# Reordering every engine's instruction list in a decoder-layer kernel, and splitting the row transfers of the softmax maxima over two queues

## The reference, cut to what matters

```python
x = layernorm(x + attention(x))       # 16 heads of 32, causal softmax, biases, output projection
x = layernorm(x + wkv(x, ctx))        # a recurrence over the tokens, channel by channel
x = layernorm(x + gated_attention(x)) # 16 query heads, one key head and one value head picked per token
```

## Time and profile before

| | us |
|---|---|
| median of 3 runs | 1542.65 (1542.21 to 1544.36) |
| the profiled execution | 1540.05 |
| its span, first to last instruction | 1538.2 |
| PE busy in the span | 1403.6 |
| DVE busy in the span | 1088.6 |
| ACT busy in the span | 647.1 |
| POOL busy in the span | 391.6 |

### The profile page before, as it was taken

How to read it: one execution, slowest core, us unless ns; L and a number is a source line. 1 busy time by engine, 2 the same in 40 slices (tenths; PEclk the granted TensorE clock), 3 DMA queues, 4 the chain that set the end, 5 groups by cost and what they waited for, 6 DMA issues and landing times.

```text
span 1538.2 us, 26567 instructions
## 1 busy us (share of the span) xinstructions
PE 1403.6 (91%) x9858; PEld 1117.2 (73%) x9858; DVE 1088.6 (71%) x2258; ACT 647.1 (42%) x1459; POOL 391.6 (25%) x520
## 2 busy tenths in 40 slices
PE   7877899999999999999999999999999999998686
PEld 6665777877777777778777777777777777775564
DVE  4464777677777767777777777777777777777744
ACT  3442525445352544535353453525345352534122
POOL 1243312222231222213122231313223131312200
PEclk9988999999999999999999999999999999999898
DMA  6431333314133331414233241333324132331110
GB/s 180 151 83 42 90 77 80 94 34 111 45 90 91 80 94 45 112 36 100 78 87 94 54 108 36 90 77 91 90 56 105 39 87 77 91 77 33 32 44 27
DMA packets 63199, 119.50 MB, mean 78 GB/s; under 512 B 14304, under 2 KB 32736, under 8 KB 63072
## 3 DMA queue, kind: packets, MB, share of 16 engines
q1 hardware_dynamic: 60128, 112.03, 29.0%
q10 hardware_dynamic: 2944, 5.77, 1.1%
HBM read 32.81 MB, written 8.39 MB: 27 GB/s over the span
## 4 chain that ended last, share of the span: by engine, by line
PE 62%; DVE 13%; ACT 9%; issue 3%; SPq 2%; DMA 2%; POOL 0%; ACTq 0%; POOLq 0%; DVEq 0%
PE pp L467 7%; PE pp L469 6%; PE pp L468 6%; PE po L572 6%; PE pw L467 4%; PE pw L469 4%; PE pw L468 4%; DVE neg_max L1499 3%; PE po L586 3%; PE po L576 3%; PE sk L545 3%; PE sk L492 3%; ACT prob L1128 3%; PE sq L507 2%; PE sq L492 2%
## 5 line engine op out<-in xcount | busy, mean ns | idle before, releaser
L1128 ACT ACTIVATE prob<-sk 128x512 f32<-128x512 f32 x384 | 215.6, 597 | 274.4 <-PE sk L492 271.5
L1499 DVE TENSOR_REDUCE neg_max<-sq 128x2 f32<-128x512 f32 (+1 forms) x384 | 252.0, 683 | 87.3 <-PE sq L492 83.6
L467 PE MATMUL pp<-xt_hi,w_hi 128*128 128x256 f32 x616 | 190.2, 309 | 12.7 <-DVE w_lo L1486 7.7
L468 PE MATMUL pp<-xt_lo,w_hi 128*128 128x256 f32 x616 | 175.2, 284 | 0.0
L469 PE MATMUL pp<-xt_hi,w_lo 128*128 128x256 f32 x616 | 175.2, 284 | 0.0
L1139 ACT ACTIVATE o_ch<-po 128x512 f32<-128x512 f32 x128 | 76.2, 596 | 162.1 <-PE po L576 160.6
L467 PEld LDWEIGHTS pp<-xt_hi,w_hi 128*128 128x128 f32 x616 | 119.7, 194 | 15.0 <-issue 11.4
L492 PE MATMUL sq<-mask_qk,ident_b 128*128 128x256 bf16 (+1 forms) x384 | 124.7, 325 | 0.0
L492 PE MATMUL sk<-mask_kq,ident_b 128*128 128x256 bf16 (+1 forms) x384 | 124.4, 324 | 0.0
L468 PEld LDWEIGHTS pp<-xt_lo,w_hi 128*128 128x128 f32 x616 | 119.3, 194 | 0.7
L469 PEld LDWEIGHTS pp<-xt_hi,w_lo 128*128 128x128 f32 x616 | 118.7, 193 | 0.0
(11 more groups left out here) (201 smaller groups left out, 3771.7 us busy)
## 6 DMA issues: line engine op xcount, KB each, us to landing
q_stack<-q_hi SPq DMA_DIRECT2D x256, 128.0 KB, 2.4
q_stack<-q_lo SPq DMA_DIRECT2D x128, 128.0 KB, 2.4
k_stack<-k_hi SPq DMA_DIRECT2D x128, 128.0 KB, 2.3
x_raw<-in_xT SPq DMA_DIRECT2D x16, 512.0 KB, 3.8
k_stack<-k_lo SPq DMA_DIRECT2D x64, 128.0 KB, 2.3
x<-in_x SPq DMA_DIRECT2D x16, 512.0 KB, 4.5
w_val<-in_ctxT SPq DMA_DIRECT2D x64, 128.0 KB, 2.2
out_y<-x SPq DMA_DIRECT2D x13, 512.0 KB, 2.8
```

The lines of the kernel that those rows point to most:

```text
L467: T.matmul(out, lh, rh, start=(c == 0), stop=False, skip_group_check=True)
L468: T.matmul(out, lh, rl, start=False, stop=False, skip_group_check=True)
L1128: A.activation(dst, sk[n % 2][:], ACT.Exp, scale=SCALE).then_inc(s_exp, 1)
L1499: V.tensor_reduce(dst, src, AX.X, ALU.max, negate=True).then_inc(s_max, 1)
```

## The change: what it does

It changes these things, and nothing that is computed:

1. **Rows of the maxima.** `row_hi` on ACT, after its copy of the high part, waits for the copy's own completion and issues the DMA of row 96 from ACT's queue. `stack_max` on SP issues row 97 alone.
2. **Passes of the loop.** PA_WO waits for six of the seven jobs, and PA_WO + 1 for the seventh. On PE `max_a(t, 1)` stands behind `sq_a(t, 1, 2)` and `sk_a(t, 0, 2)`, tiles 0 and 1 of `sk_f` ahead of `turn_f(b, 0)`, and `sk_f(b, 0, ...)` is laced in at two places. On DVE `maxima_a(t, 0, 2)` comes ahead of `recurrence_start(r, 2)`, both splits of x2 and the maxima of group 1 change places with their neighbours, and the last residual and the statistics of b - 1 stand behind them. On ACT `carry_exps(r, 2)` comes behind the exponentials of group 0 and the second row, and `exps_f(b, 2, 0, 1)` ahead of `qk_hi`. On SP `max_f(b, 3)` comes ahead of the q stacks of the next batch.
3. **Opening.** Chunks 2 and 3 of the recurrence of batch 0 move into pass 1, as in the other passes. PE issues extra matmuls that nobody reads (`keep`): 20 ahead of the first scores of batch 1, 6 ahead of those of batch 2, and 24 in pass 1. SP stacks k ahead of the context loads.
4. **Ending.** All five lists are written anew: the third sublayer of batch 14 is laced with that of batch 15 from its projections on. `kf_stack` and `logit_t` no longer share memory, the second jobs of batch 15 use `pw` in place of `po`, and the links of batches 14 and 15 have semaphores of their own.

```diff
-            def stack_max(b, g, job, s_mhi, s_free, mrow):
-                wait(sp, s_mhi, NG * b + g + 1)
-                for part in range(2):
-                    if part:
-                        wait(sp, s_free, job + 1)
-                    row = 3 * HD + part
-                    sp.dma_start(q_stack[row:row + 1, ...], max_rows[:, part, :]...).then_inc(mrow[g], 16)
+            def stack_max(b, g, job, s_free, mrow):
+                wait(sp, s_free, job + 1)
+                row = 3 * HD + 1
+                sp.dma_start(q_stack[row:row + 1, ...], max_rows[:, 1, :]...).then_inc(mrow[g], 16)
...
                 A.activation(max_rows[:, 0, :], pt[0:HG * TT, 0:P], ACT.Copy).then_inc(s_mhi, 1)
+                act.wait_ge(s_mhi, done)
+                row = 3 * HD
+                act.dma_start(q_stack[row:row + 1, ...], max_rows[:, 0, :]...).then_inc(mrow[g], 16)
...
                     if job == PA_WO:
+                        wait(pe, pf_free, PF_JOBS * (b - 1) - 1)
+                        pe.wait_ge(a_free, A_JOBS * (b + 1))
+                    if job == PA_WO + 1:
                         wait(pe, pf_free, PF_JOBS * (b - 1))
-                        pe.wait_ge(a_free, A_JOBS * (b + 1))
...
@@ TensorE, iteration
-                sq_a(t, 1, 2)
...
                 sk_a(t, 0, 0, 1)
+                sq_a(t, 1, 2)
+                sk_a(t, 0, 2)
                 max_a(t, 1)
-                sk_a(t, 0, 2)
...
-                    project_a(t, PA_WO + 1, first_scores_f)
+                    project_a(t, PA_WO + 1, {1: first_scores_f, 2: first_scores_f_end})
...
                 def second_scores_f():
                     if f:
+                        sk_f(b, 1, 0, 1)
                         turn_f(b, 0)
                         sq_f(b, 2, 2)
-                        sk_f(b, 1, 0, 1)
                         sk_f(b, 1, 2)
...
@@ ScalarE, iteration
-                if t > 1:
-                    carry_exps(r, 2)
                 value_out(t, 1)
...
                 exps_a(t, 0, 0, 1)
+                exps_a(t, 0, 2)
                 row_hi_a(t, 1)
-                exps_a(t, 0, 2)
-                if t > 1:
-                    now_exps(r, 2)
-                    carry_exps(r, 3)
+                carry_exps(r, 2)
+                now_exps(r, 2)
                 copy_a(t, 0)
-                if t > 1:
-                    now_exps(r, 3)
+                carry_exps(r, 3)
+                now_exps(r, 3)
...
+                if f:
+                    exps_f(b, 2, 0, 1)
                 qk_hi(t + 1, PA_Q + 1)
                 if f:
-                    exps_f(b, 2, 0, 1)
                     exps_f(b, 2, 2)
...
@@ VectorE, iteration
-                if t > 1:
-                    recurrence_start(r, 2)
                 maxima_a(t, 0, 2)
-                if t > 1:
-                    recurrence_start(r, 3)
+                recurrence_start(r, 2)
                 rows_a(t, 0)
-                if b >= 1:
-                    last_third_residual(b - 1, x_of(b - 1))
+                recurrence_start(r, 3)
                 maxima_a(t, 1, 0, 1)
                 if f:
                     x2_split_lo(b, 0)
-                    x2_split_lo(b, 1)
                 maxima_a(t, 1, 2)
+                if f:
+                    x2_split_lo(b, 1)
+                if b >= 1:
+                    last_third_residual(b - 1, x_of(b - 1))
                 if b >= 1:
                     third_stats(b - 1, x_of(b - 1))
                 rows_a(t, 1)
...
@@ SyncE, iteration
                 if b >= 0:
+                    max_f(b, 3)
                     q_stacks(t + 1, PA_JOBS, PA_Q, pa_free, range(NG - 2), f_sk, TILES * b, a_stk)
-                    max_f(b, 3)
...
@@ VectorE, opening
+                qk_lo(1, PA_K)
+                qk_lo(1, PA_K + 1)
                 sums(0, 0)
                 sums(0, 1)
-                recurrence_start(0, 2)
-                qk_lo(1, PA_K)
                 divide(0, 0)
-                qk_lo(1, PA_K + 1)
+                maxima_a(1, 0, 0, 1)
                 divide(0, 1)
-                recurrence_start(0, 3)
-                sums(0, 2)
-                sums(0, 3)
-                divide(0, 2)
-                divide(0, 3)
-                maxima_a(1, 0, 0, 1)
...
@@ TensorE, ending (b is 13, n is 14, then b is 15)
+                project_f(n, PF_Q, lambda: sk_f(b, 2, 0, 1))
...
+                project_f(n, PF_K + 1, lambda: turn_f(b, 3))
+                project_f(n, PF_V)
+                key_transpose(n, f_free, F_JOBS * n)
+                y_transpose(LAST, 1)
...
+                max_f(n, 0)
+                sq_f(n, 1, 0, 1)
+                b = LAST
+                x2_transpose(b)
+                sq_f(n, 1, 2)
...
+                project_f(b, PF_Q, lambda: sk_f(n, 0, 0, 1))
...
+                project_f(b, PF_Q + 1, second_scores)
...
+                project_f(b, PF_K, third_values)
+                turn_f(n, 2)
+                project_f(b, PF_K + 1, lambda: sk_f(n, 3, 0, 1))
+                sk_f(n, 3, 2)
+                project_f(b, PF_V, lambda: values_f(n, 3))
+                turn_f(n, 3)
                 key_transpose(b, f_free, F_JOBS * b)
...
@@ ScalarE, ending, batch 15: new place of the norm and store of batch 14
                 exps_f(b, 1, 2)
                 copy_f(b, 1)
+                third_norm(n, x_of(n))
+                store_whole(n)
                 exps_f(b, 2, 0, 1)
...
@@ VectorE, ending, batch 15
                 rows_f(b, 2)
+                third_stats(n, x_of(n))
                 maxima_f(b, 3)
```

More of the change, by code:

```diff
@@ L221, in build @@
         dve_a, dve_w, dve_f, dve_once = sem("dve_a"), sem("dve_w"), sem("dve_f"), sem("dve_once")
+        dve_f_end = [sem(f"dve_f_end{i}") for i in range(2)]
         pool_w, pool_once, act_once = sem("pool_w"), sem("pool_once"), sem("act_once")
@@ L718, in project_f @@
                 bank = bank_f(b, job)
-                if bank is po and job == PF_Q + 1:
-                    pe.wait_ge(f_norm, NG * b)
                 if bank is pw and job == PF_K + 1:
                     pe.wait_ge(u_free, U_JOBS * (b + 1))
+                    if b == LAST - 1:
+                        pe.wait_ge(w_free, W_JOBS * (b + 1) + W_YJ + 1)
                 else:
-                    if bank is pw and job == PF_V + 1:
+                    if bank is pw and job == PF_V + 1 and not is_last(b):
                         pe.wait_ge(w_free, W_JOBS * (b + 2))
@@ L863, in iteration @@
                 else:
+                    keep(pp, 6)
                     third_values()
+                    keep(pp, 6)
                 turn_a(t, 2)
@@ L953, in iteration @@
                     pe.wait_ge(a_max, TILES * (t + 1))
+                    keep(sq[0], 6)
                 sq_a(t + 1, 0, 0, 1)
@@ L1406, in ending @@
                 row_hi_f(b, 2)
+                carry_exps(LAST, 0)
                 copy_f(b, 1)
-                x2_split_hi(LAST - 1)
-                carry_exps(LAST, 0)
+                x2_split_hi(n)
+                carry_exps(LAST, 1)
                 exps_f(b, 2, 0, 1)
-                carry_exps(LAST, 1)
                 now_exps(LAST, 0)
-                fq_hi(LAST - 1, 0)
+                now_exps(LAST, 1)
+                fq_hi(n, 0)
                 exps_f(b, 2, 2)
-                now_exps(LAST, 1)
+                row_hi_f(b, 3)
                 copy_f(b, 2)
-                row_hi_f(b, 3)
-                fq_hi(LAST - 1, 1)
+                carry_exps(LAST, 2)
+                fq_hi(n, 1)
+                carry_exps(LAST, 3)
                 exps_f(b, 3, 0, 1)
+                now_exps(LAST, 2)
                 exps_f(b, 3, 2)
+                now_exps(LAST, 3)
+                gate_sums(n)
                 copy_f(b, 3)
-                carry_exps(LAST, 2)
-                now_exps(LAST, 2)
-                carry_exps(LAST, 3)
-                now_exps(LAST, 3)
+                row_hi_f(n, 0, f_mrow[NG - 1], 32 * n)
                 third_norm(b, x_of(b))
-                act.wait_ge(x3_ready, b + 1)
-                act.dma_start(out_d[b].rearrange("(c p) d -> p c d", p=P), x_of(b)[:]).then_inc(stored, 16)
-                b = LAST - 1
-                gate_sums(b)
+                store_whole(b)
+                b = LAST
+                x2_split_hi(b)
+                exps_f(n, 0, 0, 1)
+                for stk in f_stk:
+                    act.wait_ge(stk, 48 * b)
+                fq_hi(b, 0)
+                row_hi_f(n, 1)
+                exps_f(n, 0, 2)
+                copy_f(n, 0)
+                exps_f(n, 1, 0, 1)
+                fq_hi(b, 1)
+                exps_f(n, 1, 2)
+                row_hi_f(n, 2)
+                copy_f(n, 1)
+                exps_f(n, 2, 0, 1)
+                exps_f(n, 2, 2)
+                gate_sums(b)
+                row_hi_f(n, 3)
+                copy_f(n, 2)
+                exps_f(n, 3, 0, 1)
+                exps_f(n, 3, 2)
+                copy_f(n, 3)
```

347 lines of the change are left out of this document (157 added, 190 removed).

## The result

The changed kernel takes 1530.33 us (median of 5 runs, 1527.12 to 1533.29) where the one before took 1542.21 beside it (5 runs, 1538.30 to 1544.36): the ratio is 0.9928 [0.9905, 0.9951]. It is faster, by 12 us where I had forecast 47, and the time lies 0.3 us above my range.

What follows compares the result with a forecast made beforehand. PE, busy for 91% of the span, sets the pace, so only its waits can be gained. Loop 28.7, opening 6 and ending 12.5 us take 47.2 off 1540.05; with 2.6 added for the median, 1495.5 us, range 1474 to 1530.

Steps and rivals of the forecast that it cites:

- The loop, forecast 28.7 us: Loop: 2.55 us a pass gained from shorter PE waits, 0.5 charged for ACT, net 2.05 over 14 passes.
- I counted 2.3 of them: Loop waits of PE: 0.5 us a pass off for picked, 1.1 for maxima, 0.7 for exponentials.
- The price of the split: Loop, ACT: issuing high rows there costs 0.5 us a pass on the path, bounds 0 and 5.3.
- The 0.25 us for the rows: Loop: PE's waits for row DMAs shrink by an estimated 0.25 us a pass, the low row starting sooner.
- PA_WO's 0.5 us: Loop: of PA_WO's 1.17 us wait for picked, about 0.5 us a pass is gained; sq limits the rest.
- the waits move, and the loop gains little: Rival, loop: each removed wait shows the next DVE or ACT chain; 7 us instead of 28.7, 1517 us; 17%.
- the signs that I named as wrong: Profile after: sk and po waits for prob above 12 us, new sq waits for maxima, or pass 1 above 47 us.
- the one for ScalarE's issues: Sign in the loop that ACT's issues are on the path: sk and po wait for prob above 12 us.
- The opening, forecast 6: Opening: 7.2 us of waits and 4.3 of clock gained, 4.4 and 1 charged; bounds -2 and 14.
- the 8.7 us of which I took half: Opening: two stretches at 1.2 GHz would save 8.7 us at 2.4; 4.3 counted for keep matmuls and shorter waits.
- The ending and the tail, forecast 14 and -1.5: Ending: 9 us idle time and 5 us clock gained; tail: 1.5 us charged for batch 14's norm, store and statistics.
- The new wait of `pw`: Ending: PF_K + 1 of batch 14 waits 2.7 us for pw, freed after batch 15's second residual; the longest wait.

Runs made afterwards that it cites:

- the split alone: The kernel before the change, with only the high rows issued from ScalarE and SP issuing row 97 alone: 1557.20 us against 1543.50.
- The kernel with the load first: The changed kernel with only load_weight(W_O), the output projection's weights, ahead of the first high row on ScalarE in the opening: 1531.01 us.
- `out_lo` early: The changed kernel with out_lo(t, 0) ahead of divide(r, 2) on DVE: 1508.22 us.
- PA_WO alone: The kernel before the change, with only PA_WO's wait eased to six jobs and the seventh awaited at PA_WO + 1: 1538.92 us against 1543.50.

## Why the prediction was wrong

**The loop, forecast 28.7 us: the term that failed.** Its gains were there. The waits for picked, for exponentials and for the maxima's transposes went, 3.4 us a pass, where I counted 2.3 of them. Three steps in between failed, the first two the largest:

- *An edit that was not costed.* "The change part by part" passes over `sums(r, 2)` and `sums(r, 3)`, each one place back on DVE. I asked of each wait that went whether its own releaser was late, and not what now stood between the last maximum and `k_lo`, which frees the same bank `pt`. Taking `out_lo` out from behind the division, which shortens that chain from 3.96 to 2.31 us, gave back 1.5 us a pass, some 20 us. The scans themselves were not put back, so that their move made the wait is read from the two timelines.
- *The price of the split.* I put 0.5 us a pass on ScalarE's own path, "where `carry_exps` now stand behind the exponentials of group 0". No exponential waits there. It costs 0.68 us a pass net, elsewhere: ScalarE's issue delays `xt_hi`, that POOL's `xt_lo`, that DVE's `v_f`, that the maximum, and that PE. I looked at what PE awaits of ScalarE, not at what POOL awaits. The trace before could have shown it: `v_f` took 0.47 us beside a 0.24 of the same shape. The bounds I gave (0 and 5.3) held it. The 0.25 us for the rows was right, 0.2 measured.
- *PA_WO's 0.5 us.* I had the mechanism, `sq` behind the first maximum. (The 935.05 in that working stands in no row; the maximum's first half ends at 934.97.) Alone it gains 0.34. It counts on a maximum that comes no later, and the split takes that away: with both, `sq` waits 1.7 us.

And one term was missing: the sum has no dips of the clock in the loop. Without the 7.0 us of the three passes that hold one, the loop would have gained a little; with them it lost 3.6.

The rival "the waits move, and the loop gains little" is what came, at a price above its own: it had still left 7 us of gain in the loop. Its reason, DVE without a gap around the picks, was the right row to look at, and 17% was too little for it. Of the signs that I named as wrong, its own came, 22.2 us of new waits of `sq` for a maximum; the one for ScalarE's issues, waits for `prob`, did not.

**The opening, forecast 6, measured 9.4 from the first to the second PA_WO.** The clock (third number from the end in these rows of the two kernels) went from 0.85 to 1.00, so by my working it gave back all the 8.7 us of which I took half (no run shows the clock's part by itself):

```profile
64.50:142.00 77.50, 58.70 (x366) 46.20 (x365) 39.94 (x72) 31.82 (x72) 30.71 (x33) 0.85 0.25 62
```

```profile
69.00:137.00 68.00, 55.54 (x410) 44.91 (x408) 39.45 (x72) 31.77 (x72) 30.18 (x33) 1.00 0.29 71
```

The wait for the first maximum is gone, and that for k is 1.6 us at most (3.2 before). On the other side stand up to 4.4 us before the first PA_WO, which I had at nothing, because the first 65 us have no edit of their own but the split.

**The ending and the tail, forecast 14 and -1.5, measured 17.7 and -8.3.** The sum was 9.4, where I had 12.5. The new wait of `pw` for the second residual of 15 was forecast at 2.7 us and is the longest single one:

```profile
PE pw L483 <- DVE x L1610: 3.5, 1, 3.5
```

In the tail I charged ScalarE's norm and store at 1.5 us. What failed is the size: moving norm and store with the statistics gave 5.3 us, 3.4 by their durations and the rest with a higher clock. The rows on ScalarE, which I had credited there, cost another 1.4 (the means of 48.5 against 47.2 and 48.9 against 47.3). Why they do is not shown: under the old ending the split alone has a tail of 38.7 us, no longer than the 40.2 before. The last 1.6 us stay open.

**The rule I weighed.** The issue on ScalarE takes 0.63 us, within my bounds. The Trainium skill (DMA: Bandwidth & Descriptors, "Issuing engines are not separate DMA queues") says that such a split saves only sequencer time, usually little. The trace agrees on the size: 0.2 us a pass, 2.6 us in 13, where no maximum stands behind it.

## What to carry to other kernels

When a wait is taken out of a full pipeline, list everything else that frees the same bank or feeds the next instruction, on every engine, and ask it of each moved instruction in the diff, the ones that look neutral too. An issue moved to an engine with idle time is not free if something behind it on that engine starts a chain on a third one: follow it until it meets the critical engine again. An instruction that is sometimes longer than the same form elsewhere is a row to explain before it is built upon; and a part that costs, like this split, shows only when the parts are timed alone.

## What the runs showed of the hardware

**A small DVE instruction was held up by a running POOL instruction.** `v_f` (TENSOR_SCALAR, 128x32, fp32) took 0.24 us alone, and 0.47, 1.35 and 1.42 us where it began 1.95, 1.07 and 1.03 us into POOL's `xt_lo` of 2.4 us; in these three it ended 0.04 us after `xt_lo`. In the loop of the changed kernel three more kinds got longer where they began during an instruction of POOL: the TENSOR_TENSOR `k<-k_sel,k` (128x32, 0.19 us alone, 1.17 to 1.28 then), the TENSOR_TENSOR `x<-x,o_tok` (128x256, 0.42 and 0.92) and the scan `w_e<-w_e` (128x256, 0.67 alone, 0.96 to 1.21 then). Two kinds beside `xt_lo` were hardly touched: `picked<-pw`, which reads a bank, took 0.67 us during it and 0.67 to 0.69 elsewhere, and the TENSOR_REDUCE behind it 1.10 us during `xt_lo` and 1.06 outside it (medians of 13 each in the kernel before). The Trainium skill (SBUF — State Buffer, "Who interferes with whom") says that VectorE and GpSimd share one pair of ports, which is held for a whole instruction while the other blocks, and that a tensor_scalar can ask for that pair and a reduction can't. These rows agree. Here a wait on the less busy engine was worth 19 us.

**The clock.** In the loop of the changed kernel the granted clock falls to 1.2 GHz three times (at 487, 846 and 1204 us), and the passes with such a dip are 1.9 to 2.8 us longer than undisturbed ones. The kernel with the load first has three, `out_lo` early one, and in all three kernels `sq` waits 1.7 to 2.0 us in every pass. Each of these seven dips begins 0.2 to 1.7 us after the end of that wait. The wait isn't enough, since 10 of the 13 passes of the changed kernel have it and no dip, and it isn't the only cause: PA_WO alone has one dip, elsewhere in the pass. The kernel before and the other ten runs have none in the loop. The passes without a dip are not all equal either: above the shortest they have 2.1 to 7.8 us in 13 (4.5 before, 2.8 in the changed kernel), and no run explains those. Each kernel was profiled once, so what sets off a single dip stays open.
